# Mamba mixer with attention on one core: front work on other scan steps, half of the product with C on GpSimd

## The reference, cut to what matters

```
h  = concat(class token, patches @ W / 255 + b) + positions;  h = concat(h, text)     # 274 tokens x 192
xn = layernorm(h)
for direction in (forward, backward):
    xi, z = split(xn @ in_proj);   xc = silu(causal_conv4(xi));   dt_lo, B, C = split(xc @ x_proj)
    dt = softplus(dt_lo @ dt_w + dt_b)
    s[t] = exp(dt[t] * A) * s[t-1] + dt[t] * xc[t] * B[t];   y[t] = sum_n C[t, n] * s[t, n] + D * xc[t]
    mixed += (y * silu(z)) @ out_proj
h = h + layernorm(xn + mixed) * g + b
h = h + block(layernorm(h))     # attention with 12 heads and an MLP; the second 16 images
                                # ("small") add three gated variants of the projection and the MLP
```

## Time and profile before

| | us |
|---|---|
| median of 3 runs | 5700.33 |
| lowest and highest | 5692.26, 5709.53 |
| the profiled execution | 5727.32 |
| its span, first to last instruction | 5725.5 |

### The profile page before, as it was taken

One profiled execution on the slowest core, in us unless ns is written; L12 is line 12 of the kernel. 1 busy time (PEld: TensorE's weight loads), 2 busy tenths in 40 slices (PEclk: granted clock), 3 DMA queues, 4 the chain that ended last, 5 costly groups with the idle time before them and its releaser, 6 DMA issues.

```text
span 5725.5 us, 69728 instructions
## 1 busy us (share of the span) xinstructions
PE 4406.4 (77%) x23852; PEld 2476.2 (43%) x23852; DVE 4944.8 (86%) x3712; ACT 3172.3 (55%) x6914; POOL 1.5 (0%) x9
## 2 busy tenths in 40 slices
PE   3577778777777877777778787788778877787877
PEld 2244444444344444444444444444445444444433
DVE  4999998999999899999998988888987889888971
ACT  2455555555565555555556655555555655556642
POOL 0000000000000000000000000000000000000000
PEclk7677888887788878877888878887877878888876
DMA  5877787778778777877786786777766677676840
GB/s 143 206 170 172 175 198 179 177 172 188 178 164 192 182 178 170 194 176 164 178 191 162 168 186 149 165 165 163 169 152 163 159 178 162 155 176 163 178 101 3
DMA packets 182843, 953.92 MB, mean 167 GB/s; under 512 B 26557, under 2 KB 76157, under 8 KB 84042
## 3 DMA queue, kind: packets, MB, share of 16 engines
q1 hardware_dynamic: 182442, 948.83, 72.2%
HBM read 888.14 MB, written 60.60 MB: 166 GB/s over the span
## 4 chain that ended last, share of the span: by engine, by line
PE 37%; DVE 36%; issue 14%; DMA 7%; ACT 5%; DVEq 1%; SPq 0%; ACTq 0%; POOL 0%; POOLq 0%
DVE hs L1084 15%; DVE hs L1090 6%; DVE hs L1073 5%; PE f_ps L675 4%; DMA h<-in_txt 3%; PE a_ps L516 3%; DVE neg_max L1178 3%; PE f_ps L639 3%; PE f_ps L686 2%; PE f_ps L629 2%; PE y_ps L480 2%; PE f_ps L556 2%; PE a_ps L526 2%; PE f_ps L581 2%; DVE xc L1142 2%
## 5 line engine op out<-in xcount | busy, mean ns | idle before, releaser
L1084 DVE TENSOR_TENSOR_SCAN hs<-decay,hs 128x2192 f32<-128x2192 f32 x384 | 1810.5, 4715 | 27.6 <-ACT decay L832 27.5
L832 ACT ACTIVATE decay<-decay,a_cols 128x273 f32<-128x273 f32 x3072 | 1369.0, 511 | 0.4
L1090 DVE TENSOR_TENSOR hs<-hs,c_s 128x2192 f32<-128x2192 f32 x384 | 933.5, 2431 | 56.0 <-issue 56.0
L1073 DVE TENSOR_TENSOR hs<-hs,b_ps 128x2192 f32<-128x2192 f32 x384 | 930.4, 2423 | 17.1 <-DMA hs<-dtu_rows 17.1
L924 ACT ACTIVATE hid<-f_ps 92x1096 f32<-92x1096 f32 x288 | 310.9, 1079 | 649.4 <-PE f_ps L629 649.1
L480 PE MATMUL y_ps<-hs,y_pick 128*32 128x274 f32 x6144 | 554.5, 490 | 55.4 <-DVE hs L1090 55.4
L516 PE MATMUL a_ps<-xn,w_in_s 96*128 96x274 f32 x1536 | 514.6, 463 | 98.0 <-ACT zs L855 50.5
L1178 DVE TENSOR_REDUCE neg_max<-f_ps 92x4 f32<-92x1096 f32 x288 | 371.5, 1290 | 185.9 <-PE f_ps L621 185.9
L629 PE MATMUL f_ps<-hid 32*92 32x274 f32 x1536 | 189.5, 573 | 339.5 <-DVE neg_max L1178 329.8
L516 PEld LDWEIGHTS a_ps<-xn,w_in_s 96*128 96x128 f32 x1536 | 319.2, 219 | 275.7 <-ACT zs L855 77.6
L480 PEld LDWEIGHTS y_ps<-hs,y_pick 128*32 128x32 f32 x6144 | 185.4, 127 | 374.8 <-issue 241.8
(11 more groups left out here) (149 smaller groups left out, 5927.9 us busy)
## 6 DMA issues: line engine op xcount, KB each, us to landing
decay<-dt_rows SPq DMA_DIRECT2D x384, 1096.0 KB, 9.0
hs<-dtu_rows SPq DMA_DIRECT2D x384, 1096.0 KB, 12.8
dt_rows<-dt SPq DMA_DIRECT2D x192, 137.0 KB, 10.0
dtu_rows<-dtu SPq DMA_DIRECT2D x192, 137.0 KB, 9.8
xp<-in_patches SPq DMA_DIRECT2D x32, 588.0 KB, 19.5
out<-h SPq DMA_DIRECT2D x32, 205.5 KB, 2.2
h<-in_txt SPq DMA_DIRECT2D x32, 57.8 KB, 11.7
w_in_s<-in_w_in SPq DMA_DIRECT2D x1, 1152.0 KB
```

Of the source, the lines that this page charges most:

```text
L832: e = act.activation(dec[:, k, t], dec[:, k, t], ACT.Exp, scale=a_cols[:, d * IC + u, TILES * half + k:TILES * half + k + 1])
L1073: dve.tensor_tensor(x[:, :, :], x[:, :, :], b_ps[:, 0:T].unsqueeze(1).broadcast_to([128, TILES, T]), ALU.mult).then_inc(dbu_done, 1)
L1084: dve.tensor_tensor_scan(i, a, i, 0.0, ALU.mult, ALU.add).then_inc(scan_done, 1)
L1090: dve.tensor_tensor(x[:, :, :], x[:, :, :], c_s[d][:, :].unsqueeze(1).broadcast_to([128, TILES, T]), ALU.mult).then_inc(hc_done, 1)
```

## The change

- `output_product` on DVE keeps tiles 0 to 3 of the 8; a new loop on POOL, the same for every step of every image, multiplies tiles 4 to 7 by C once the scan is done and C is copied. PE's sum over the states, and ACT's next copy of C, wait for both.
- The in-projection of direction 1 is split: its xi half is made in gaps 14 to 16 of direction 1 of the image before (for the first image ahead of the loop), its z half in gaps 0 to 2 of direction 0. The projection of the next image's direction 0 moves by one gap, to gaps 1 to 6 of direction 1. The copies to the z buffer wait for the gating unit by unit.
- The convolution of direction 1 moves from gaps 3, 5, 7 to 1, 3, 5; its silu from gap 8 to 6, x_proj from 10 to 7, step widths from 11 to 13 to 8 to 10, C from 14 to 11. For direction 0 of the next image x_proj, step widths and C come one gap sooner (9, 10 to 12, 13).
- The embedding moves from gaps 6 and 7 of direction 0 to 15 and 16, its addition to 16, mean, centring and squares from 8 to 17, variance, root and scaling from 9 and 10 to gap 0 of direction 1.

```
-        CONV_GAPS = ((3, 5, 7), (4, 5, 7))
-        XP_GAP = 10
-        DT_GAPS = (11, 12, 13)
-        C_GAP = 14
+        POOL_TILE = 4
+        CONV_GAPS = ((1, 3, 5), (4, 5, 7))
+        SILU_GAPS = (6, 8)
+        XP_GAPS = (7, 9)
+        DT_GAPS = ((8, 9, 10), (10, 11, 12))
+        C_GAPS = (11, 13)
         B_GAP = 15
+        X_AHEAD_GAP = 14
+        TOK_GAPS = (15, 16)
+        TOK_ADD_GAP, MEAN_GAP = 16, 17
+        A_VAR_GAP = XN_GAP = 0
...
         # POOL
+            def output_product(b, q):
+                d, x = q // 6, hs[q % 4][:, POOL_TILE:TILES, :]
+                pool.wait_ge(c_copied, at(b, 2, d + 1))
+                pool.wait_ge(scan_done, at(b, SCANS, q + 1))
+                pool.tensor_tensor(x, x, c_s[d][:, :].unsqueeze(1).broadcast_to([128, TILES - POOL_TILE, T]),
+                                   ALU.mult).then_inc(hc_pool, 1)
+            def step(b, f, e, a):
+                for q in range(SCANS):
+                    output_product(b, q)
...
         # PE
             def sum_states(b, q):
                 wait(pe, hc_done, at(b, SCANS, q + 1))
+                wait(pe, hc_pool, at(b, SCANS, q + 1))
...
             def fronts(b, d, a, gap):
-                x, xd = (b, 1) if d == 0 else (a, 0)
-                if x is not None:
-                    if gap < 2 * IC:
-                        in_proj(x, xd, gap, gap + 1)
-                if d == 0 and a is not None and gap == 6:
+                if d == 0 and gap < IC:
+                    in_proj(b, 1, IC + gap, IC + gap + 1)
+                if d == 0 and a is not None and gap == TOK_GAPS[0]:
                     tok(a, (0,))
+                if d == 1 and a is not None:
+                    if 1 <= gap <= 2 * IC:
+                        in_proj(a, 0, gap - 1, gap)
+                    if 0 <= gap - X_AHEAD_GAP < IC:
+                        in_proj(a, 1, gap - X_AHEAD_GAP, gap - X_AHEAD_GAP + 1)
...
         # ACT
-                    if j == IC:
-                        wait(act, gated, at(ago(b, 1), UNITS, IC * (d + 1)))
+                    if j >= IC:
+                        wait(act, gated, at(ago(b, 1), UNITS, IC * d + j - IC + 1))
...
             def c_copy(b, d):
                 act.wait_ge(c_mm, at(b, 2, d + 1))
                 wait(act, hc_done, at(b, SCANS, 6 * d - 6))
+                wait(act, hc_pool, at(b, SCANS, 6 * d - 6))
...
         # DVE
-                dve.tensor_tensor(x[:, :, :], x[:, :, :], c_s[d][:, :].unsqueeze(1).broadcast_to([128, TILES, T]),
+                x = x[:, 0:POOL_TILE, :]
+                dve.tensor_tensor(x, x, c_s[d][:, :].unsqueeze(1).broadcast_to([128, POOL_TILE, T]),
                                   ALU.mult).then_inc(hc_done, 1)
...
+                            if d == 1 and j == 0:
+                                wait(dve, ysum, at(b, SCANS, -1))
```

More of the change, by code:

```diff
@@ L258, in build @@
         hc_done = sem("hc_done")
+        hc_pool = sem("hc_done_by_pool")
         ysum = sem("ysum")
@@ L461, in _ @@
             pool.memset(v_mask[0:1, 1:3], 0.0).then_inc(s_cp, 1)
+            def output_product(b, q):
[7 more added lines that the diff above has]
+                    output_product(b, q)
+            program(step, pool.Fori, lambda: None, lambda f, e: None)
         @block.tensor
@@ L488, in tok @@
                 if not first(b):
-                    pe.wait_ge(xz_copied, at(ago(b, 1), 12, 12))
+                    pe.wait_ge(c_copied, at(ago(b, 1), 2, 2))
                 for i in halves:
@@ L522, in x_proj_mm @@
                 pe.wait_ge(silu_done, at(b, 4, 2 * d + 1))
-                if d == 1 and not last(b):
-                    pe.wait_ge(a_ln, at(b, 1, 2))
                 for k in range(IC):
@@ L742, in fronts @@
             def fronts(b, d, a, gap):
-                x, xd = (b, 1) if d == 0 else (a, 0)
-                if x is not None:
-                    if gap < 2 * IC:
-                        in_proj(x, xd, gap, gap + 1)
-                if d == 0 and a is not None and gap == 6:
-                    tok(a, (0,))
+                if d == 0 and gap < IC:
+                    in_proj(b, 1, IC + gap, IC + gap + 1)
+                if d == 0 and a is not None and gap == TOK_GAPS[0]:
+                    tok(a, (0,))
+                if d == 1 and a is not None:
[3 more added lines that the diff above has]
+                        in_proj(a, 1, gap - X_AHEAD_GAP, gap - X_AHEAD_GAP + 1)
             def fronts_early(b, d, a, gap):
                 x, xd = (b, 1) if d == 0 else (a, 0)
-                if x is not None and gap == XP_GAP:
+                if x is not None and gap == XP_GAPS[d]:
                     x_proj_mm(x, xd)
-                if x is not None and gap in DT_GAPS:
-                    dt_mm(x, xd, DT_GAPS.index(gap))
-                if x is not None and gap == C_GAP:
+                if x is not None and gap in DT_GAPS[d]:
+                    dt_mm(x, xd, DT_GAPS[d].index(gap))
+                if x is not None and gap == C_GAPS[d]:
                     c_spread(x, xd)
@@ L760, in fronts_early @@
                 if d == 0 and a is not None:
-                    if gap == 7:
+                    if gap == TOK_GAPS[1]:
                         tok(a, (1,))
-                    if gap == 8:
+                    if gap == MEAN_GAP:
                         a_mean_mm(a)
-                    if gap == 9:
-                        a_var_mm(a)
+                if d == 1 and a is not None and gap == A_VAR_GAP:
+                    a_var_mm(a)
             def step(b, f, e, a):
@@ L804, in front @@
                 b_spread(b, 0)
+                in_proj(b, 1, 0, IC)
             def finish(f, e):
@@ L998, in fronts @@
                 x, xd = (b, 1) if d == 0 else (a, 0)
+                if d == 0 and 1 <= gap <= IC:
+                    xz_copy(b, 1, IC + gap - 1, IC + gap)
+                if d == 1 and a is not None:
+                    if 2 <= gap <= 2 * IC + 1:
+                        xz_copy(a, 0, gap - 2, gap - 1)
+                    if 1 <= gap - X_AHEAD_GAP <= IC:
+                        xz_copy(a, 1, gap - X_AHEAD_GAP - 1, gap - X_AHEAD_GAP)
                 if x is not None:
-                    if 1 <= gap <= 2 * IC:
-                        xz_copy(x, xd, gap - 1, gap)
-                    if gap == 8:
+                    if gap == SILU_GAPS[d]:
                         silu(x, xd)
-                    if gap == XP_GAP:
+                    if gap == XP_GAPS[d]:
                         xproj_copy(x, xd)
-                    if gap in DT_GAPS:
-                        dt_parts(x, xd, DT_GAPS.index(gap))
-                    if gap == C_GAP:
+                    if gap in DT_GAPS[d]:
+                        dt_parts(x, xd, DT_GAPS[d].index(gap))
+                    if gap == C_GAPS[d]:
                         c_copy(x, xd)
-                if d == 0 and a is not None and gap == 9:
+                if d == 1 and a is not None and gap == A_VAR_GAP:
                     rstd(a_ps[0:CH, 0:T], rstd_a, a_var, at(a, 1, 1), a_ln, at(a, 1, 1), a_rstd)
             def fronts_late(b, d, a, gap):
-                if d == 0 and a is not None and gap == 8:
+                if d == 0 and a is not None and gap == MEAN_GAP:
                     squares(xn[parity(a)][:, :, :], sq_a, a_cen, at(a, 1, 1), a_sq)
@@ L1049, in front @@
                 c_copy(b, 0)
+                xz_copy(b, 1, 0, IC)
                 act.wait_ge(s_ac, 1)
@@ L1275, in fronts @@
                         conv(x, xd, (CONV_GAPS[d].index(gap),))
-                    if gap - 1 in DT_GAPS:
-                        dt_sum(x, xd, DT_GAPS.index(gap - 1))
+                    if gap - 1 in DT_GAPS[d]:
+                        dt_sum(x, xd, DT_GAPS[d].index(gap - 1))
                 if d == 0 and a is not None:
-                    if gap == 7:
+                    if gap == TOK_ADD_GAP:
                         tok_add(a)
-                    if gap == 8:
+                    if gap == MEAN_GAP:
                         centre(h[parity(a)], xn[parity(a)], a_ps[0:CH, 0:T], a_mean, at(a, 1, 1), a_cen)
-                    if gap == 10:
-                        scale_by(xn[parity(a)], xn[parity(a)][:, :, :], rstd_a, a_rstd, at(a, 1, 1), xn_ready)
+                if d == 1 and a is not None and gap == XN_GAP:
+                    scale_by(xn[parity(a)], xn[parity(a)][:, :, :], rstd_a, a_rstd, at(a, 1, 1), xn_ready)
             def step(b, f, e, a):
```

## The result

The changed kernel takes 5856.43 us (median of 4 runs, 5849.52 to 5862.82), the kernel before 5700.55 beside it: 1.0273 of its time, 95% interval 1.0253 to 1.0293, 156 us slower. The forecast was 5481 us, faster. The profiled execution took 5857.8 us, its span is 5856.0.

The account below looks back on a forecast made before the run. DVE was taken to bound most steps, PE those around the old projection and embedding. From 5727 us the terms gave 5341, with 166 of interference 5507, scaled to a median of 5481 us (range 5310 to 5670).

Parts of the forecast that it names:

- The product, -438 us: DVE's product with C, halved from 2431 to 1290 ns, relieves DVE of 1.14 us 384 times, as far as DVE bounds.
- step 9: The division waits for ACT, with step-width activations now ahead, so DVE's saved time only lengthens the wait: +84 us.
- the small images: DVE already waits for PE in step 1, so the savings of steps 0 and 1 are lost in 16 images: +36 us.
- My rival of waiting: Saved time becomes waiting, only six of twelve steps gain: 5709 us, or 5682 as a median, about no change; chance 0.11.
- Interference, +166 us: DVE instructions with two SBUF inputs stand still beside POOL's product behind scans: 5.2 us an image, 32 images.
- my middle of the bounds: POOL's half product was taken at 1.9 us, between bounds of 1.0 and 2.8 us from POOL's other instructions.
- The moved work: Terms for moved projections, embedding and their followers; the +3 is three projections made ahead of the first scan.
- The centring: Centring of the new embedding no longer waits for the mean, following a product with B: -69 us.
- step 3: The first row maximum's scores lose the matmuls and activations queued ahead; 2.6 us in 31 images: -80 us.
- 2.5 us an image for steps 4 to 6: PE makes the embedding between scores there, so DVE may wait 0 to 5.3 us; 2.5 taken: +78 us.
- scores that make DVE wait by more than 5 us: Sign that the forecast is wrong: scores behind the moved embedding make DVE wait by more than 5 us.
- The slower rival: POOL's product outlasts its cover, DVE's half waits; loses from 3.0 us, at 4 us 5975, median 5947; chance 0.14.

Follow-up runs that it names:

- run 2: The changed kernel's new schedule alone, with DVE making the whole product and POOL nothing: 5778.49 us, 1.0101 of the kernel before.
- run 3: The changed kernel without POOL's instruction and the waits on it, tiles 4 to 7 not multiplied by C: 5669.78 us, 0.9903 of the kernel before.
- run 4: The kernel before with DVE multiplying only tiles 0 to 3 by C and nobody tiles 4 to 7: 5581.23 us, 0.9765.
- Run 5: The changed kernel with six extra matmuls on PE at the end of gap 19: 5698.00 us, 0.9965 of the kernel before.
- run 12: The new schedule with the whole product on DVE, POOL nothing, and six extra matmuls on PE: 5618.67 us, 0.9844 of the kernel before.
- run 10: The changed kernel with POOL started by DVE's product with B, plus six extra matmuls at the end of gap 19: 5419.95 us, 0.9500.

## Why the prediction was wrong, step by step

- **The product, -438 us "as far as DVE bounds": the step that failed.** The size of the relief was right (427 and 422 us of busy time); that it would nearly all show was not: from run 2 to run 3 the time falls by 109 us, from the kernel before to run 4 by 139. That is the larger part of the miss. The forecast adds up to -438 + 166 + 52 = -220 us; the runs give -109 for the half left out, +187 for POOL and +58 for the schedule, together +136 (156 were measured; the 20 between are those by which the kernel before differs in the two sets of runs). Of the 356 us between the two, the product is 329. In the old schedule with half left out (mean lengths, large images from the fourth to the sixteenth), steps 7, 8 and 10 lose exactly 1.14 us, while steps 1, 2, 3, 6 and 9 grow by 0.5 to 1.3: their ends are set mostly by PE and ACT (in step 1 partly by a load), and DVE comes there earlier only to wait. I had charged this only in step 9 and in the small images. A busy share of 93% in a large image (152.4 of 163.5 us) does not say that DVE ends last in 93% of it. My rival of waiting named this, at 0.11, and priced it without interference.
- **Interference, +166 us.** The mechanism was right and the size too low: DVE's instructions are 288 us longer in all, and the time grows by about 187. POOL takes 2.34 us and not 1.9; the convolution behind a scan loses 1.94 us and not 1.5; and scalings from SBUF to SBUF are slowed too, one that I had taken as cover (L1149, by 52.7 us) and one that I had not counted (L1196, by 28.7). DVE's timeline of the changed kernel, the scan and two convolutions, and POOL's product:

```profile
1700.95 4.71 DVE L1116 TENSOR_TENSOR_SCAN hs<-decay,hs 128x2192 f32<-128x2192 f32 x1
1705.58 0.40 DVE L1173 TENSOR_SCALAR xc<-xi,inner_s 128x274 f32<-128x274 f32 x1
1706.01 3.52 DVE L1177 SCALAR_TENSOR_TENSOR xc<-xi,inner_s,xc 128x274 f32<-128x274 f32 x3
1709.44 2.43 DVE L1105 TENSOR_TENSOR hs<-hs,b_ps 128x2192 f32<-128x2192 f32 x1
1711.79 0.42 DVE L1173 TENSOR_SCALAR xc<-xi,inner_s 128x274 f32<-128x274 f32 x1
1712.24 1.58 DVE L1177 SCALAR_TENSOR_TENSOR xc<-xi,inner_s,xc 128x274 f32<-128x274 f32 x3
```

```profile
1705.74 2.41 POOL L475 TENSOR_TENSOR hs<-hs,c_s 128x1096 f32<-128x1096 f32 x1 [15.62 <-DVE hs L1116]
```

  The same three multiply-adds take 3.52 us while POOL works (to 1708.15) and 1.58 after it. The difference, 1.94 us, is nearly all of the 2.14 us that POOL's product still had to go when they began at 1706.01. That agrees with the Trainium skill, "SBUF — State Buffer", section "Who interferes with whom": two SBUF inputs of VectorE meet GpSimd's reads, and the second to come stands still until the first is done. My estimate of 2.41 us from the Trainium skill, "GPSIMD Engine Reference", section 3.1, was nearer to the measured 2.34 than my middle of the bounds.
- **The moved work, -69 - 80 + 78 + 84 + 36 + 3 = +52 us.** The schedule alone measures +58 in time, +53 in span, and this agreement is accidental. The centring did lose its wait (68.8 to 4.3 us), but in the small images DVE now waits about as long at the next place in step 2, a sum (`res<-f_ps,gate,res`) whose idle time grows from 69.1 to 127.5 us, so the gain was only in part real. Wrong: step 3 hardly changed in the large images (17.72 to 17.95 us in the mean), and step 9 became shorter (15.18 to 14.00), its wait moved from the division (163 to 44 us) to the sums of step widths. Missed altogether: step 6, 4.7 us longer. I had charged 2.5 us an image for steps 4 to 6, where these three grow by 6.3 together (large images again), by counting PE's free microseconds, which take the same matmul to cost the same.
- **PE's clock, in no term of the sum.** In step 6 of the changed kernel PE has done its queue and waits 3.7 us; what follows runs at 1.2 GHz, and DVE waits for it. Before, PE was busy 11.8 of the 13.0 us of that step at a clock of 0.90, in the image from which the earlier trace rows are, and its wait at the same place was 1.22 us. Run 5 shows the cause: only the wait was filled, and 158 us came back. I had named scores that make DVE wait by more than 5 us as a sign of being wrong; it came true in step 6 (6.8 us), and mostly by the clock: with the wait filled it is 2.0. With the six matmuls, the schedule by itself is worth -96 us (run 12), and the half product under B on top of it another 199 (run 10). The window of step 6 before, and PE's scores behind the maximum in it:

```profile
1321.10:1334.10 13.00, 11.78 (x91) 6.20 (x89) 12.16 (x7) 7.93 (x20) 0.00 (x0) 0.90 0.95 217
```

```profile
1327.05 0.71 PE L629 MATMUL f_ps<-qk 32*92 32x274 f32 x8 [1.22 <-DVE neg_max L1178]
```

- **The slower rival** gave the right sign by a mechanism that did not decide: POOL's product, 2.34 us, stays below the 3.0 us from which it was to lose, and DVE's half behind the product with B kept its 1.29 us.

## What to carry to other kernels

Before work is taken from the fullest engine, ask at each step which wait ends last there; in this kernel a saved microsecond was a microsecond only in steps where that engine hardly waits. Work given to GpSimd beside VectorE did no harm here under a product of VectorE that reads one input from PSUM, tied to it by a semaphore; started whenever its data were ready, it landed on the convolution. And where TensorE alternates with another engine, moving matmuls out of its way can lower its granted clock and lengthen the chain that remains, as in step 6: read the clock of every step in the windows, not only the busy time.

## What the runs showed of the hardware that I had not expected

- Six matmuls more made a kernel 158 us faster, because the chain behind them in step 6 ran at 2.4 instead of 1.2 GHz; the same six in the old schedule, whose wait at that place is short, cost about 96 us.
- POOL's product slowed also DVE's scaling with one SBUF input (416 to 826 ns in the mean), not only two-input instructions; yet the convolution's first multiplication, in which POOL's product starts, kept its 0.40 us.
- POOL's two-input product of 1096 columns takes 2.32 us with nothing in its way, 1.8 times DVE's 1.29.
